# Causal attention loop: value products of two steps together, four buffers for the kept value sums

## The reference

```
qkv = x @ w_qkv                       # 2048 x 384, split into q, k, v of 16 heads x 8
scores = q @ k.T * (1 / sqrt(8))      # per head, 2048 x 2048
attn = softmax(scores, axis=-1)       # first attention: causal, second: full
out = attn @ v                        # per head, 2048 x 8
```

## Time and profile before

| | |
|---|---|
| timed runs | 1310.21, 1313.02, 1321.1 us |
| the profiled execution | 1324.03 us, its span 1322.2 us |
| granted clock of TensorE, mean | 0.987 |
| PE busy | 1249.8 us, 95% |
| DVE busy | 1147.4 us, 87% |
| ACT busy | 1062.1 us, 80% |
| POOL busy | 184.0 us, 14% |
| causal loop | steps from 95 to 471 us |
| full attention's loop | values from 659 to 1247 us |

### The profile page before, as it was taken

One profiled execution on the slowest core, in us unless ns is written; L12 is line 12 of the kernel. 1 busy time (PEld: TensorE's weight loads), 2 busy tenths in 40 slices (PEclk: granted clock), 3 DMA queues, 4 the chain that ended last, 5 costly groups with the idle time before them and its releaser, 6 DMA issues. The chain is left out here.

```text
span 1322.2 us, 30389 instructions
## 1 busy us (share of the span) xinstructions
PE 1249.8 (95%) x11960; PEld 453.6 (34%) x12022; DVE 1147.4 (87%) x1528; ACT 1062.1 (80%) x2064; POOL 184.0 (14%) x463
## 2 busy tenths in 40 slices
PE   7887999999999989899899999999999999999998
PEld 3252332333233343455322233322333323333454
DVE  6776989899999657766999999999999999998375
ACT  4556877898899956534599999999999999999741
POOL 9233221111111110110200000000000000000000
PEclk9898999999999999999999999999999999999999
DMA  5243220500000003000422000000000000000000
GB/s 133 57 130 51 34 36 14 60 12 4 13 4 4 4 11 82 15 0 25 129 55 61 4 4 13 2 4 4 13 4 3 3 4 13 4 3 3 12 9 24
DMA packets 38525, 35.11 MB, mean 27 GB/s; under 512 B 16080, under 2 KB 31920, under 8 KB 38384
## 3 DMA queue, kind: packets, MB, share of 16 engines
q1 hardware_dynamic: 38384, 33.17, 11.1%
HBM read 17.03 MB, written 9.70 MB: 20 GB/s over the span
## 5 line engine op out<-in xcount | busy, mean ns | idle before, releaser
L1577 DVE TENSOR_REDUCE m_blockmax<-ps 128x2 f32<-128x1024 f32 (+1 forms) x768 | 873.7, 1208 | 32.5 <-PE ps L1390 17.6
L1541 ACT ACTIVATE m_prob<-ps 128x512 f32<-128x512 f32 (+3 forms) x1664 | 849.2, 575 | 45.4 <-PE ps L1428 36.4
L1428 PE MATMUL ps<-m_q_max,m_k_all 64*128 64x512 bf16 (+3 forms) x1664 | 333.7, 367 | 2.5 <-issue 2.0
L1390 PE MATMUL ps<-m_k_all,m_q_all 64*128 64x512 bf16 (+2 forms) x1732 | 320.4, 374 | 16.2 <-DVE m_blockmax L1577 13.0
L1451 PE MATMUL ps<-m_prob,m_v_op 128*9 128x256 f32 x4096 | 317.0, 381 | 0.1
L1390 PEld LDWEIGHTS ps<-m_k_all,m_q_all 64*128 64x128 bf16 x1732 | 81.7, 92 | 331.4 <-DVE m_blockmax L1577 222.7
L1447 PE MATMUL ps<-m_prob,m_v_op 128*9 128x256 f32 (+3 forms) x2560 | 179.3, 352 | 8.9 <-ACT m_pv L1515 6.9
L1428 PEld LDWEIGHTS ps<-m_q_max,m_k_all 64*128 64x128 bf16 x1664 | 146.8, 94 | 89.6 <-ACT m_prob L1541 38.5
L1600 POOL CAST m_maxparts<-m_negmax 128x8 bf16<-128x8 f32 x64 | 14.1, 220 | 701.8 <-DVE m_negmax L1556 696.5
L1451 PEld LDWEIGHTS ps<-m_prob,m_v_op 128*9 128x9 f32 x4096 | 60.9, 88 | 130.0 <-issue 118.9
L829 ACT ACTIVATE m_prob<-ps 128x512 f32<-128x512 f32 x40 | 23.9, 596 | 62.9 <-PE ps L692 54.3
(11 more groups left out here) (231 smaller groups left out, 969.8 us busy)
## 6 DMA issues: line engine op xcount, KB each, us to landing
m_part<-m_xn SPq DMA_DIRECT2D x48, 128.0 KB, 2.3
ba_parts<-m_part SPq DMA_DIRECT2D x8, 384.0 KB, 5.4
ea_parts<-m_part SPq DMA_DIRECT2D x8, 384.0 KB, 2.6
m_k_all<-ea_parts SPq DMA_DIRECT2D x84, 32.0 KB
m_q_all<-ea_parts SPq DMA_DIRECT2D x84, 32.0 KB
m_k_all<-ba_parts SPq DMA_DIRECT2D x36, 64.0 KB
m_q_all<-ba_parts SPq DMA_DIRECT2D x36, 64.0 KB
ba_sums<-m_pv SPq DMA_DIRECT2D x128, 9.0 KB
```

The costliest lines, as they stand in the source:

```text
L1390: mm = pe.matmul(ps[:, MX + 2 * (u % 2) + j, 0:width], q_all[head, pair, q0:q0 + TW], k_all[head, pair, CW * kc:CW * kc + width], start=Tr ...
L1428: pe.matmul(ps[:, e % ST, q0:CW], k_all[head, pair, TW * i:TW * i + TW], q_max[m % 2][head, q0:CW], start=True, stop=True).then_inc(self.s ...
L1541: nc.scalar.activation(prob[:, (2 * t + j) % NP, q0:CW], ps[:, e % ST, q0:CW], ACT.Exp, scale=SCALE)\
L1577: nc.vector.tensor_reduce(blockmax[:, m % plan.AHEAD, qt, :, kc], ps[:, MX + 2 * (u % 2):MX + 2 * (u % 2) + 2, 0:width], AX.X, ALU.max)\
```

## The change

Three edits. First, in the causal loop the value products stand behind every second step (odd step numbers), for the steps three and two before it; the full attention keeps its order. Second, `by_values` moves the turn of the maxima so that it stands directly behind such an odd step, if there are eight places between it and the window's last fill; otherwise behind the next odd step. For c > 0 this is one step earlier than before (behind the step with 384 columns instead of the one with 256). Third, there are four buffers for the kept sums: the two of before and the last quarter of `cen`, which holds the low parts of k until POOL is done with them (the added wait, for the third window). Both attentions count the sends on the same four semaphores.

```diff
         for n in range(2, self.count):
             at = order.index(("turn", n, 0))
-            if order[at - 1][0] != "fill":
+            if order[at - 1][0] == "exp" and self.step_no[order[at - 1][1:]] % 2 == 1:
                 continue
-            after = next(i for i in range(at, len(order)) if order[i][0] == "exp")
-            if order[after][1] < n:
-                order.insert(after, order.pop(at))
+            odd = [i for i, o in enumerate(order) if o[0] == "exp" and self.step_no[o[1:]] % 2 == 1]
+            filled = order.index(("fill", n, self.keys(n) - 1))
+            behind = max(i for i in odd if i < at)
+            if behind < filled + 8:
+                behind = min(i for i in odd if i > at)
+            if order[behind][1] < n:
+                order.insert(behind + (1 if behind < at else 0), order.pop(at))
...
+    KEPT = 4
...
-        self.sums_sent = [n.sem(f"sums_sent{a}") for a in range(2)]
+        self.sums_sent = [n.sem(f"sums_sent{a}") for a in range(self.KEPT)] if earlier is None else earlier.sums_sent
+        self.sent_base = 0 if earlier is None else 16 * 4 * (plan.count // self.KEPT)
+        last = chunk(k["cen"], NC - 1)
+        self.kept = [k["sums"][:, 0, :], k["sums"][:, 1, :], last[:, 0:HALF_CW], last[:, HALF_CW:CW]]
...
                 scores(m, i)
-                if plan.step_no[m, i] >= plan.delay:
-                    sum_values(plan.step_no[m, i] - plan.delay)
-        for t in range(len(plan.steps) - plan.delay, len(plan.steps)):
+                t = plan.step_no[m, i]
+                if causal and t % 2 == 1 and t >= plan.delay:
+                    sum_values(t - plan.delay)
+                    sum_values(t - plan.delay + 1)
+                elif not causal and t >= plan.delay:
+                    sum_values(t - plan.delay)
+        for t in range(len(plan.steps) - 2, len(plan.steps)):
             sum_values(t)
...
             act.wait_ge(self.pv_done, plan.last_step(m) + 1)
-            if m >= 2:
-                act.wait_ge(self.sums_sent[m % 2], 16 * 4 * (m // 2))
-            nc.scalar.activation(sums[:, m % 2, :], ps[:, SUM, 0:HALF_CW], ACT.Copy).then_inc(self.sums_ready, 1)
+            if m == 2:
+                act.wait_ge(self.lo_ready, 2 * NC)
+            if m >= self.KEPT:
+                act.wait_ge(self.sums_sent[m % self.KEPT], self.sent_base + 16 * 4 * (m // self.KEPT))
+            nc.scalar.activation(self.kept[m % self.KEPT], ps[:, SUM, 0:HALF_CW], ACT.Copy).then_inc(self.sums_ready, 1)
...
-                    source = sums[row:row + HD + 1, m % 2, :]
+                    source = self.kept[m % self.KEPT][row:row + HD + 1, :]
...
-                    sp.dma_start(into, source).then_inc(self.sums_sent[m % 2], 16)
+                    sp.dma_start(into, source).then_inc(self.sums_sent[m % self.KEPT], 16)
...
-            for a in range(2):
-                sp.wait_ge(self.sums_sent[a], 16 * 4 * (PAIRS // 2) * (c + 1))
+            for a in range(self.KEPT):
+                sp.wait_ge(self.sums_sent[a], self.sent_base + 16 * 4 * (PAIRS // self.KEPT) * (c + 1))
```

More of the change, by code:

```diff
@@ L1508, in act_loop @@
         nc, ps, k, plan, ST, SUM, NP = self.nc, self.ps, self.k, self.plan, self.ST, self.SUM, self.NP
-        prob, q_max, sums = k["prob"], k["q_max"], k["sums"]
+        prob, q_max = k["prob"], k["q_max"]
         def keep_sums(m):
             act.wait_ge(self.pv_done, plan.last_step(m) + 1)
-            if m >= 2:
-                act.wait_ge(self.sums_sent[m % 2], 16 * 4 * (m // 2))
-            nc.scalar.activation(sums[:, m % 2, :], ps[:, SUM, 0:HALF_CW], ACT.Copy).then_inc(self.sums_ready, 1)
+            if m == 2:
[3 more added lines that the diff above has]
+            nc.scalar.activation(self.kept[m % self.KEPT], ps[:, SUM, 0:HALF_CW], ACT.Copy).then_inc(self.sums_ready, 1)
         for kind, m, i in plan.order:
@@ L1626, in sp @@
         k, plan, causal = self.k, self.plan, self.causal
-        q_all, k_all, part, sums, den = (k[name] for name in ("q_all", "k_all", "part", "sums", "den"))
+        q_all, k_all, part, den = (k[name] for name in ("q_all", "k_all", "part", "den"))
         def send_parts(i):
```

## The result

The changed kernel takes 1357.32 us (median of six runs, 1353.62 to 1361.76), the kernel before 1320.21 us (six runs, the three shown ahead and three beside the changed kernel). The ratio is 1.0308, with a 95% interval from 1.0275 to 1.0340: slower by 3.1%, 41 us (the two medians are 37 us apart). The profiled execution took 1359.3 us, span 1357.5. Every ratio and median here is of undisturbed executions alone; all six of each kernel are among them.

What follows compares the result with a forecast made beforehand. Attention loops keep PE (95% busy), DVE and ACT nearly full; in pairs the wait for a score bank decides. Profiled: 1324.0 + 40.3 - 6.4 = 1357.9 us; against the median 1313.0 + 33.9 = 1347 us, range 1331 to 1361.

Steps and rivals of the forecast that it cites:

- The pair's chain: Causal loop: second odd-step score matmul waits for a bank, so a pair takes 2.59 us instead of 2.17.
- S1: The odd step's two score matmuls in a pair; the second was forecast 1.06 us behind S0.
- S0: The even step's two score matmuls, which open a pair; its first exponential frees the bank S1's second matmul needs.
- V to V: On PE, from one step's eight value matmuls (V) to the next's: 0.43 us, against 0.55 to fill matmuls (F).
- The saving on PE: Fewer switches between matmul groups on PE: 0.12 + 0.09 = 0.21 us a pair, already within the 2.59.
- Rival A: Causal loop: PE's time binds, not the bank; pairs go at DVE's pace, faster, 1291 us; chance 9%.
- The count: Causal loop: 96 pairs pay 0.42 us each, +40 us; windows' first and last pairs taken at nothing.
- The turn: Turn of the maxima moved behind the paired values: 0, from -6 to +6 us.
- The buffers: Four kept buffers remove ACT's one wait for the first send; window 8's first fill comes earlier: -6.4 us.
- B: No difference: bank's wait coincides with the fill's wait for DVE, pairs at 2.28 us; 1317 us, chance 6%.
- C: Buffers don't help: window 8's fill or a later send takes over the whole stall; 1353 us, chance 4%.
- D: PE idles more, and its clock falls to 0.50 in the loop; well over 1362 us, chance 2%.

Runs made afterwards that it cites:

- e12: Changed kernel's order with four buffers, causal fills and maxima for the first head only, and a fourth score bank; ratio to before 0.9874, 1302.3 us.
- e5: Changed kernel with 120 exponentials, the first (j = 0) of even steps from step 32, cut to half their columns; ratio to before 1.0132.
- e6: Changed kernel with 120 exponentials, the second (j = 1) of even steps from step 32, cut to half their columns; ratio to before 1.0329.
- e11: Kernel before's order with four buffers, causal fills and maxima for the first head only, and a fourth score bank; ratio to before 0.9847, 1297.7 us.
- e10: Changed kernel's order with four buffers, causal fills and maxima for the first head only, three score banks; ratio to before 1.0306, 1358.9 us.
- e3: Kernel before plus four kept buffers and values of two steps together, turns at their old places; ratio to before 1.0265.
- e1: Kernel before with four kept buffers alone, order of steps, values and turns as before; ratio 0.9984, 1313.2 us.
- e2: Kernel before plus four kept buffers and turns at their new places, values directly behind each step; ratio to before 1.0015.
- e7: Kernel of e1 (old order) with the first exponential of the same even steps as in e5 cut to half its columns; ratio to before 0.9962.
- e8: Changed kernel with the fill in front of an even step moved behind it, windows 8 and up; ratio to before 1.0178.
- e4: Kernel before with values of two steps together alone, two kept buffers, turns at their old places; ratio to before 1.0274.

## Why the prediction was right, point by point

**The pair's chain** was right to the hundredth for the pair shown: 2.59 us, S1's second matmul 1.07 us after S0, V to V 0.43 within the 0.98 of V V. Taking away the dependence (e12) takes away the loss; shortening exactly one exponential (e5) shortens the pair by what it is shorter, and its twin (e6) does nothing.

The saving on PE is real too, only smaller: with the wait gone, pairs inside a window of 16 steps take 2.00 to 2.12 us in e12, and two steps of the old order 2.17 to 2.27 us in e11. The rule of TensorEngine Tiling (Array Packing), Key Properties, in the Trainium skill, that a change of tiling mode drains the engine, agrees with the 0.12 us between V to F and V to V. Rival A, which it pointed to, did not happen. The Trainium skill's Perfetto Trace Analysis, Matmuls, names the larger one, that groups of matmuls should rotate through PSUM banks so that one is emptied while the next is computed; e10 against e12 puts 57 us on it here.

**The count** of 96 pairs was right, and 0.42 us for each was a little high: 40 us forecast, 37 measured (e3 against e1). These are the times from one even step's scores to the next one's in a window of 16 steps, from the starts of L1428, L1432 and L1436 (windows from 385.58, 384.89 and 382.89 us):

| | first pair | six full pairs | last pair |
|---|---|---|---|
| before | 1.95 | 2.23, 2.28, 2.29, 2.17, 2.02, 2.26 | 2.35 (with turn) |
| e3 | 2.06 | 2.65, 2.59, 2.70, 2.60, 2.43, 2.53 | 2.18 (with turn) |
| changed | 2.06 | 2.65, 2.59, 2.70, 2.59, 2.43, 3.09 (with turn) | 1.95 |

All six pay, between 0.27 and 0.43 us, 2.25 us together where 2.52 were forecast. The afterwards was right (2.58 us on average, 2.59 forecast), the before a little low: two steps took 2.21 us on average, not 2.17, and 2.34 us in windows of 8 steps, whose two pairs pay 0.24 us each. The first pair was taken at nothing against its own sum (2.04 against 1.94); it pays 0.11 us in every window.

**The turn**, forecast at 0 with 6 us either way, costs 5.7 us in the times (1.0308 less 1.0265, measured apart from each other, so a difference of that size is not certain by itself) and 8.3 us by the windows. It does cost PE the same 0.55 us at either place, as forecast. What the prediction overlooked is that at its old place, once steps stand in pairs, the turn lies inside the new wait: the last pair of e3 is 0.17 us shorter than before with the turn in it. In the old order, with no wait to lie in, moving it costs 0.06 us in steady windows of 16 steps and nothing in the others (e2).

**The buffers**, forecast at -6.4 us, gave -2.1 (from -5.5 to +1.2). The wait that goes and the place where a part of it comes back were right: the first fill of window 8 was named as what is late next. I allowed it 0.9 us of wait, worked out from one trace, and it was 3.3 us in the profiled execution of e1, 2.2 in e3, 0.8 in e5, 0.4 in e2, and nothing in e6, e7 and the changed kernel. In e1's profiled execution the fill came 5.1 us earlier, 1.3 less than forecast; why the times say 2.1 is open.

The three terms measured are 37.0, 5.7 and -2.1 us. They add up to the 40.7 measured because each is a difference between neighbouring kernels, so the sum confirms nothing; 33.9 was forecast. The pairs came out 3 us under their term, the turn 6 and the buffers 4 us over theirs: that the first took back a third of what the other two added is luck. That the forecast of 1357.9 for the profiled execution fits its 1359.3 better than 1347 fits 1357.3 is chance: the median of before moved from 1313.0 to 1320.2 us with more runs.

Rivals A and B are refuted (e5, e8, e12), and C was partly right in the kernel with buffers alone (e1). D's large loss did not occur: the granted clock is 1.00 in the steady windows shown. But the clock does fall in the loop, and not only after some us without any matmul, as the prediction read it. In the kernel before it fell at 218.3 us, and from 214 us on the longest idle time of PE ahead of that was 0.75 us (the row of one matmul, then the stretch around the fall):

```profile
216.96 0.28 PE L1390 MATMUL ps<-m_k_all,m_q_all 64*128 64x256 bf16 x2 [0.75 <-DVE m_blockmax L1577]
...
216.00:222.00 6.00, 4.53 (x40) 1.41 (x40) 5.73 (x9) 2.00 (x4) 0.00 (x0) 0.72 0.00 1
```

In the changed kernel it fell three times. A window with such a stretch is 0.6 us longer (c = 2, last window: 18.58 us in e4 with one, 17.94 in e3 without) to 1.3 us (c = 3, last window: 19.47 in the changed kernel, 18.19 in e3). That is some 2 or 3 us of the changed kernel's time, and the kernel before has stretches of its own. Whether the pairs bring more of them isn't shown.

## What to carry to other kernels

Before work is moved out from between two uses of a ring of buffers, write down for each use which earlier release it waits for and what ran meanwhile: here the value products were the cover of an exponential, and moving them bought 0.21 us of switching for 0.63 us of waiting. A ring of three with two uses a step left room for one step's scores here, not for two. And when a wait in an in-order queue can't be removed, ask what may stand in it: two fills there gave back 17 us, and a turn that had stood there by accident cost 0.3 to 0.4 us a window when it was tidied away.

## What the hardware showed that I had not expected

A stall taken away at one engine came back at another by a different amount in each execution: the same loads held PE for 3.3 us in e1 and not at all in e7, with the same order of instructions. Single traces of such a place are worth little; the ratio over twelve runs said 2 us.

PE also stood still with no releaser that the profile shows, at places that differ between executions. A window of e12 at c = 1 took 12.24 us among neighbours of 8.74:

```profile
159.00:167.74 8.74, 8.10 (x101) 3.46 (x98) 4.63 (x11) 7.64 (x18) 2.45 (x9) 1.00 0.57 70
167.74:179.98 12.24, 10.09 (x101) 3.69 (x99) 4.64 (x11) 7.64 (x18) 2.45 (x9) 0.86 0.18 25
```

It holds a stop of 1.51 us in the middle of the value products, up to 173.49, and from 173.0 a stretch of 3.4 us at a granted clock of 0.50, in which the same matmuls keep PE busy longer (10.09 us in the window, 8.10 in the one ahead). The kernel before has such stops too (1.99 us up to 260.94, 1.20 us up to 171.14). Their cause is open.
